# Attention outputs of a quad's two halves accumulated in one PSUM bank and evacuated once instead of twice

## The reference

```python
def _L0_attn_b_ref(x, qkv_w, qkv_b, out_w, out_b):
    H, hd = 16, 8
    qkv = (x @ qkv_w.T + qkv_b).reshape(B, S, H, 3 * hd)
    q, k, v = jnp.split(jnp.transpose(qkv, (2, 0, 3, 1)), 3, axis=2)
    scores = jnp.einsum('hbds,hbdt->hbst', q, k) / jnp.sqrt(jnp.float32(hd))
    w = jax.nn.softmax(scores, axis=-1)
    attn = jnp.einsum('hbst,hbdt->hbsd', w, v)
    ...
    return attn @ out_w.T + out_b
```

## Time and profile before

| | |
|---|---|
| median of 3 runs | 554.64 us |
| the profiled execution | 554.74 us |
| its span | 552.9 us |
| PE busy | 504.7 us (91%) |
| DVE busy | 461.9 us (84%) |
| ACT busy | 364.3 us (66%) |
| POOL busy | 101.7 us (18%) |

### The profile page before, as it was taken

How to read it: one execution, slowest core, us unless ns; L and a number is a source line. 1 busy time by engine, 2 the same in 40 slices (tenths; PEclk the granted TensorE clock), 3 DMA queues, 4 the chain that set the end, 5 groups by cost and what they waited for, 6 DMA issues and landing times.

```text
span 552.9 us, 9775 instructions
## 1 busy us (share of the span) xinstructions
PE 504.7 (91%) x3856; PEld 238.0 (43%) x3856; DVE 461.9 (84%) x649; ACT 364.3 (66%) x690; POOL 101.7 (18%) x122
## 2 busy tenths in 40 slices
PE   1994988998699999999999999999999999989797
PEld 1443465576334333333343333343343333333476
DVE  5999859987599899999999999999999999913753
ACT  1766230442101888888888888888888888898441
POOL 6974999241000000000000000000000000000000
PEclk9997989999755899999999999999999999999999
DMA  8111000004720030300300300300300000000001
GB/s 217 23 39 39 0 2 1 1 22 154 223 58 1 1 79 4 76 2 4 76 2 2 79 3 2 77 2 3 77 2 2 1 3 3 1 2 2 0 20 57
DMA packets 13786, 18.87 MB, mean 34 GB/s; under 512 B 3583, under 2 KB 10158, under 8 KB 12718
## 3 DMA queue, kind: packets, MB, share of 16 engines
q1 hardware_dynamic: 12888, 17.53, 12.1%
q0 software_dynamic: 304, 0.46, 0.5%
q10 hardware_dynamic: 550, 0.27, 0.2%
HBM read 11.70 MB, written 5.24 MB: 31 GB/s over the span
## 4 chain that ended last, share of the span: by engine, by line
PE 72%; DVE 16%; ACT 6%; DMA 3%; issue 2%; SPq 1%; ACTq 0%
PE ps L1295 27%; PE ps L1261 26%; PE pm L1031 6%; DVE acc L833 4%; PE pm L1218 3%; PE ps L1021 3%; PE pm L1021 3%; DVE mx L935 2%; ACT gate L690 2%; DVE h L749 2%; ACT o_sb L659 2%; PE ps L1245 2%; DMA kt<-k_scr 1%; DVE st L726 1%; DMA x<-in_L_attn_a_x 1%
## 5 line engine op out<-in xcount | busy, mean ns | idle before, releaser
L935 DVE TENSOR_REDUCE mx<-pm 128x1 f32<-128x1024 f32 x256 | 310.7, 1224 | 26.2 <-PE pm L1218 25.3
L1218 PE MATMUL pm<-kt,qt 62*128 62x512 f32 x512 | 198.8, 474 | 6.2 <-DVE mx L935 3.2
L1295 PE MATMUL ps<-qt,kt 64*128 64x512 f32 x496 | 182.6, 451 | 4.6 <-ACT gate L690 4.6
L690 ACT ACTIVATE gate<-ps 128x512 f32<-128x512 f32 x250 | 134.0, 599 | 17.4 <-PE ps L1295 16.1
L690 ACT ACTIVATE acc<-ps 128x512 f32<-128x512 f32 x246 | 133.7, 595 | 17.3 <-PE ps L1295 11.4
L1295 PEld LDWEIGHTS ps<-qt,kt 64*128 64x128 f32 x496 | 75.8, 186 | 99.8 <-ACT gate L690 45.3
L1218 PEld LDWEIGHTS pm<-kt,qt 62*128 62x128 f32 x512 | 82.8, 197 | 21.4 <-DVE mx L935 18.1
L1261 PE MATMUL ps<-gate,val 128*32 128x256 f32 x1024 | 82.4, 394 | 1.4 <-ACT gate L690 1.4
L1261 PE MATMUL ps<-acc,val 128*32 128x256 f32 x1024 | 78.5, 390 | 1.2 <-ACT acc L690 1.2
L478 POOL CAST mx_s<-mx 128x16 fp32r<-128x16 f32 x16 | 3.1, 196 | 273.5 <-DVE mx L935 273.5
L1261 PEld LDWEIGHTS ps<-acc,val 128*32 128x32 f32 x1024 | 21.8, 108 | 43.7 <-ACT acc L690 23.7
(11 more groups left out here) (193 smaller groups left out, 468.9 us busy)
## 6 DMA issues: line engine op xcount, KB each, us to landing
qt<-q_scr SPq DMA_DIRECT2D x32, 128.0 KB
kt<-k_scr SPq DMA_DIRECT2D x32, 128.0 KB
x<-in_L_attn_a_x SPq DMA_DIRECT2D x4, 256.0 KB, 4.8
us<-h SPq DMA_DIRECT2D x8, 128.0 KB, 2.4
q_scr<-attn SPq DMA_DIRECT2D x4, 256.0 KB, 2.8
k_scr<-attn SPq DMA_DIRECT2D x4, 256.0 KB, 4.1
q_scr<-gate SPq DMA_DIRECT2D x4, 256.0 KB, 2.7
k_scr<-gate SPq DMA_DIRECT2D x4, 256.0 KB, 3.9
```

The source lines that it names most:

```text
L690: act.activation(pexp[s % NPB][:, exp_heads(n, s)[j], :], e_bank(i), ACT.Exp, scale=SCALE).then_inc(exp_done, 1)
L935: dve.tensor_reduce(mx[:, hn % 2, u:u + 1], pm[g % MRING][:, :], AX.X, ALU.max).then_inc(m_read, 1)
L1218: mm = pe.matmul(pm[g % MRING][:, keys * CH:(keys + 1) * CH], qt[r][rows, half, pair, c * P:(c + 1) * P], kt[r][rows, keys, pair, :], star ...
L1295: pe.matmul(e_bank(i), keys, qt[r][rows, half, pair, :], start=True, stop=True).then_inc(exp_mm, 1)
```

## The change

The bank is now emptied once per quad. V is kept in rows of 41 columns (`VS = VW + HD + 1`): nine zeros, the 8 dimensions, the ones, and 23 zeros. `pv` still takes 32 columns of it as weights. In the first half it starts at column 9, so that the outputs and the sum stand in rows 0 to 8 of the head's 32 rows; in the second half it starts at column 0, so that they stand in rows 9 to 17, and nothing but zeros is added to rows 0 to 8. Both halves accumulate into the same 512 columns of bank 2, over all 16 steps. `copy_o`, `turn_o` and `copy_turned` run once per quad, at the first steps of the next quad; `copy_turned` issues two copies, one for each half's nine columns. The step s = 8 has the ordinary `ORDER`, and the ring of banks has one item less per quad. At the end VectorE copies both halves of the last quad.

```diff
--- before.py
+++ after.py
@@ -47,6 +47,7 @@
 SHIFT_ROW = ROWS - PARTS
 NBUF = 3
 VW = 32
+VS = VW + HD + 1
 EPS_LN, EPS_RMS = 1e-5, 1e-6
 SCALE = float(HD) ** -0.5
 STEPS = 2 * BT
@@ -97,7 +98,7 @@
 
     half, tile = divmod(s, BT)
     maxima = min(2 * NQ, 1 + 2 * n + half + ((tile, j) >= TURN_MAX_AT))
-    outputs = max(0, 2 * n - 1 + half + (tile >= TURN_O_AT))
+    outputs = max(0, n - 1 + (s >= TURN_O_AT))
     return (n * STEPS + s) * QH + j + maxima + outputs
 
 
@@ -113,9 +114,8 @@
     return exp_item(n, half * BT + TURN_MAX_AT[0], TURN_MAX_AT[1]) - 1
 
 
-def out_item(hn):
-    n, half = divmod(hn + 1, 2)
-    return exp_item(n, half * BT + TURN_O_AT, 0) - 1
+def out_item(n):
+    return exp_item(n + 1, TURN_O_AT, 0) - 1
 
 
 MORE_AT = (NQ - 1, LAST_UNIT_STEP + 2)
@@ -215,7 +215,9 @@
 
         qt = [sb(f"qt{r}", [P, 2, PAIRS, CH], F32R) for r in range(NBUF)]
         kt = [sb(f"kt{r}", [P, 2, PAIRS, CH], F32R) for r in range(NBUF)]
-        v4 = [val_f[:, r * BT * QH * VW:(r + 1) * BT * QH * VW].rearrange("p (c j w) -> p c j w", c=BT, j=QH)
+
+
+        v4 = [val_f[:, r * BT * QH * VS:(r + 1) * BT * QH * VS].rearrange("p (c j w) -> p c j w", c=BT, j=QH)
               for r in range(NBUF)]
 
         pexp = [gate[:, 0, :, :], gate[:, 1, :, :], acc[:, 0, :, :], acc[:, 1, :, :]]
@@ -450,7 +452,7 @@
                 pool.memset(v4[r][:, :, :, :], 0.0).then_inc(v4_zero, 1)
             pool.wait_ge(v4_zero, NBUF)
             for r in range(NBUF):
-                pool.memset(v4[r][:, :, :, HD:HD + 1], 1.0).then_inc(v4_ones, 1)
+                pool.memset(v4[r][:, :, :, 2 * HD + 1:2 * HD + 2], 1.0).then_inc(v4_ones, 1)
             pool.wait_ge(v4_ones, NBUF)
             for c in range(NCH):
 
@@ -465,7 +467,7 @@
                 if n >= NBUF:
                     pool.wait_ge(pv_mm, STEPS * (n - NBUF + 1))
                 src = v_tok[:, b * BT:(b + 1) * BT, :].rearrange("p c (g j d) -> p g c j d", g=GQ, d=HD)
-                pool.tensor_copy(v4[n % NBUF][:, :, :, 0:HD], src[:, g, :, :, :]).then_inc(v4_ready, 1)
+                pool.tensor_copy(v4[n % NBUF][:, :, :, HD + 1:2 * HD + 1], src[:, g, :, :, :]).then_inc(v4_ready, 1)
 
             def split_max(hn):
 
@@ -652,10 +654,10 @@
             first_parts(3)
 
 
-            def copy_o(hn):
-                act.wait_ge(pv_mm, hn * BT + BT)
-                if hn:
-                    act.wait_ge(exp_mm, out_item(hn - 1) + 1)
+            def copy_o(n):
+                act.wait_ge(pv_mm, n * STEPS + STEPS)
+                if n:
+                    act.wait_ge(exp_mm, out_item(n - 1) + 1)
                 act.activation(o_sb[:, :], bank(2), ACT.Copy).then_inc(o_copied, 1)
 
             def copy_max(hn):
@@ -665,26 +667,28 @@
                     act.wait_ge(shift_in, hn * SHIFT)
                 act.activation(nm_s[:, :], e_bank(max_item(hn))[0:PARTS * HT, 0:P], ACT.Copy).then_inc(exp_done, 1)
 
-            def copy_turned(hn):
-
-                n, half = divmod(hn, 2)
-                act.wait_ge(exp_mm, out_item(hn) + 1)
-                src = e_bank(out_item(hn)).rearrange("p (c j w) -> p c j w", c=TC, j=QH)
-                dst = attn[:, n, :, :].rearrange("p d (j c) -> p c j d", j=QH)[:, TC * half:TC * (half + 1), :, :]
-                act.activation(dst, src[:, :, :, 0:HD + 1], ACT.Copy).then_inc(exp_done, 1)
+            def copy_turned(n):
+
+                act.wait_ge(exp_mm, out_item(n) + 1)
+                src = e_bank(out_item(n)).rearrange("p (c j w) -> p c j w", c=TC, j=QH)
+                dst = attn[:, n, :, :].rearrange("p d (j c) -> p c j d", j=QH)
+                for half in range(2):
+                    ins = act.activation(dst[:, TC * half:TC * (half + 1), :, :],
+                                         src[:, :, :, (HD + 1) * half:(HD + 1) * (half + 1)], ACT.Copy)
+                ins.then_inc(exp_done, 1)
 
             def quad(n):
                 for s in range(STEPS):
                     half, tile = divmod(s, BT)
-                    if tile == TURN_O_AT and (n or half):
-                        copy_turned(n * 2 + half - 1)
+                    if n and s == TURN_O_AT:
+                        copy_turned(n - 1)
                     if n or s >= NPB:
                         act.wait_ge(pv_mm, n * STEPS + (s - NPB + 1))
                     for j in range(QH):
                         if (tile, j) == TURN_MAX_AT and n * 2 + half + 1 < 2 * NQ:
                             copy_max(n * 2 + half + 1)
-                        if (tile, j) == COPY_O_AT and (n or half):
-                            copy_o(n * 2 + half - 1)
+                        if n and (s, j) == COPY_O_AT:
+                            copy_o(n - 1)
                         i = exp_item(n, s, j)
                         act.wait_ge(exp_mm, i + 1)
                         act.activation(pexp[s % NPB][:, exp_heads(n, s)[j], :], e_bank(i), ACT.Exp,
@@ -696,7 +700,7 @@
                 act.wait_ge(scr_done[i], 2 * STORED)
             for n in range(NQ):
                 quad(n)
-            copy_o(2 * NQ - 1)
+            copy_o(NQ - 1)
 
             stds(3, 0)
             stds(3, 1)
@@ -936,7 +940,7 @@
 
             def sums(quads):
 
-                dve.wait_ge(exp_done, out_item(2 * quads[-1] + 1) + 1)
+                dve.wait_ge(exp_done, out_item(quads[-1]) + 1)
                 q = slice(quads[0], quads[-1] + 1)
                 settled(dve.reciprocal(o_rc[:, q, :], attn[:, q, HD, :]))
 
@@ -968,10 +972,13 @@
             projected(1)
 
             dve.wait_ge(o_turned, 1)
-            dve.wait_ge(exp_done, out_item(2 * NQ - 2) + 1)
             o = bank(4).rearrange("p (c j w) -> p c j w", c=TC, j=QH)
-            dst = attn[:, NQ - 1, :, :].rearrange("p d (j c) -> p c j d", j=QH)[:, TC:2 * TC, :, :]
-            settled(dve.tensor_copy(dst, o[:, :, :, 0:HD + 1]))
+            dst = attn[:, NQ - 1, :, :].rearrange("p d (j c) -> p c j d", j=QH)
+            for half in range(2):
+                dve.tensor_copy(dst[:, TC * half:TC * (half + 1), :, :],
+                                o[:, :, :, (HD + 1) * half:(HD + 1) * (half + 1)]).then_inc(dve_step, 1)
+            steps[0] += 2
+            dve.wait_ge(dve_step, steps[0])
             settled(dve.reciprocal(o_rc[:, NQ - 1, :], attn[:, NQ - 1, HD, :]))
             flatten(2, [GQ - 1])
             flatten(3, [GQ - 1])
@@ -1235,14 +1242,14 @@
                 pe.transpose(e_bank(max_item(hn))[0:PARTS * HT, 0:P], mx_s[:, hn % 2, :],
                              ident[:, :]).then_inc(exp_mm, 1)
 
-            def turn_o(hn):
-
-                pe.wait_ge(o_copied, hn + 1)
-                last = hn == 2 * NQ - 1
+            def turn_o(n):
+
+                pe.wait_ge(o_copied, n + 1)
+                last = n == NQ - 1
                 if not last:
-                    item_free(out_item(hn))
+                    item_free(out_item(n))
                 for t in range(TC):
-                    mm = pe.transpose((bank(4) if last else e_bank(out_item(hn)))[:, t * P:(t + 1) * P],
+                    mm = pe.transpose((bank(4) if last else e_bank(out_item(n)))[:, t * P:(t + 1) * P],
                                       o_sb[:, t * P:(t + 1) * P], ident[:, :])
                 mm.then_inc(o_turned if last else exp_mm, 1)
 
@@ -1253,14 +1260,14 @@
                     pe.wait_ge(exp_done, exp_item(n, s, QH - 1) + 1)
                     if s == 0:
                         pe.wait_ge(v4_ready, n + 1)
-                    hn = n * 2 + s // BT
-                    if s % BT == 0 and hn:
-                        pe.wait_ge(o_copied, hn)
+                        if n:
+                            pe.wait_ge(o_copied, n)
+                at = 0 if s // BT else HD + 1
                 cols = slice(part * (CH // 2), (part + 1) * (CH // 2))
                 for j in range(QH):
-                    mm = pe.matmul(bank(2)[VW * j:VW * (j + 1), cols], v4[r][:, s % BT, j, :],
-                                   pexp[s % NPB][:, j, cols], start=(s % BT == 0 and part == 0),
-                                   stop=(s % BT == BT - 1 and part == 1), tile_position=(0, VW * j))
+                    mm = pe.matmul(bank(2)[VW * j:VW * (j + 1), cols], v4[r][:, s % BT, j, at:at + VW],
+                                   pexp[s % NPB][:, j, cols], start=(s == 0 and part == 0),
+                                   stop=(s == STEPS - 1 and part == 1), tile_position=(0, VW * j))
                 if part == 1:
                     mm.then_inc(pv_mm, 1)
 
@@ -1277,12 +1284,12 @@
                     j = 0
                     if tile == 0:
                         pe.wait_ge(shift_in, (hn + 1) * SHIFT)
-                    if tile == TURN_O_AT and hn:
-                        turn_o(hn - 1)
+                    if n and s == TURN_O_AT:
+                        turn_o(n - 1)
                     if n == NQ - 1 and s in PROJECT_AT:
                         pe.wait_ge(m_read, UNITS)
```

(4 more changed lines are left out.)

## The result

| | before | changed |
|---|---|---|
| median of 6 runs | 554.78 us | 548.58 us |
| lowest to highest | 553.9 to 555.49 | 547.36 to 551.19 |
| the profiled execution | 554.74 us | 547.36 us |
| its span | 552.9 us | 545.6 us |

The ratio to the kernel before is 0.9892, 95% interval 0.9867 to 0.9916: 6 us faster. The kernel before has three runs more here than in the table ahead of the prediction. The forecast was 547.8, range 546.4 to 550.6. In the changed kernel's listing the lines stand a few numbers lower than before: L1295 is now L1302, L1218 is L1225, L1261 is L1268, L690 is L694, L935 is L939, L659 is L661, L1245 is L1252, L674 is L676, L974 is L978.

The account below looks back on a forecast made before the run. TensorE was taken to set the attention's pace, with VectorE some 7% in reserve. The terms -6.3 - 0.85 + 0.35 = -6.8 us led from the median of 554.64 to 547.8 us, range 546.4 to 550.6.

Parts of the forecast that it names:

- VectorE has a reserve and TensorE sets the pace: In the attention, VectorE can take a reduction per 1.14 us but gets one per 1.229; some 7% in reserve.
- 0.90 us per evacuation, seven times, -6.3 us: Inner evacuations of quads 0 to 6 go; each costs 0.44 + 0.59 - 0.13 = 0.90 us in the TensorE-paced stretch.
- Why the 0.44 us gap is there: VectorE's gap at a half boundary: TensorE waits 0.30 us for ScalarE, late because of the 0.60 us bank copy.
- -0.85 us in the last quad: Eighth inner evacuation, at 492 us with no maxima left: two steps' excess of 0.52 + 0.33; bounds 0.3 and 1.3.
- Second copy on ScalarE hidden, 0: Transposed output's second copy at seven outer boundaries adds 0.33 us of ScalarE time, covered: 0, at most 3.1 us.
- +0.35 us for the second copy at the end: At the attention's end VectorE copies two halves instead of one, on the path; bounds 0.2 and 0.41 us.
- Weight loads unchanged, 0: Loads of `pv` weights from 41-float rows at unaligned starts stay at 108 ns: 0, upper end 19.5 us.
- this rival: Padded V slows the first weight loads of 256 `pv` parts; 27 ns eats the gain, 76 ns gives 567.3 us; chance 0.05.
- GpSimd's longer memsets, 0: Memsets of V grow from 2.76 to 3.5 us, followed by 8.80 us of idle time, so nothing shows.
- its first rival: The doubled copy on ScalarE comes onto the path at outer boundaries: 550.9 us at worst, 549.3 at half; chance 0.08.

Follow-up runs that it names:

- e1_transposes: The changed kernel plus four 128x128 transposes on TensorE per quad, beside the maxima's transpose at step 5; ratio 0.9957 to the kernel before.
- e4_order_first: The changed kernel with the boundary order of letters kept at the inner boundaries, where nothing is emptied any more; ratio 0.9919 to the kernel before.

## Why the prediction was right, step by step

- **VectorE has a reserve and TensorE sets the pace**: right. e1_transposes adds TensorE time alone, and the expected 0.44 us a time appears as 0.43.
- **0.90 us per evacuation, seven times, -6.3 us**: right in size. In the same V layout it is 0.89, -6.2; the trace of the changed kernel shows -5.92, since the layout costs 0.28.
- **Why the 0.44 us gap is there**: wrong. I read the 0.30 us wait of TensorE as the lateness that the copy causes. Taking the copy away and keeping the order (e4_order_first) leaves the gap at 0.44 and the wait at 0.21. Two thirds of this part, 0.20 of 0.29, come from the order of letters and the ring of three banks. That this did no harm to the number is luck: the change removed the order along with the copy. Had the diff left `ORDER_FIRST` at s = 8, my sum would have been 1.4 us too good.
- **-0.85 us in the last quad**: right, 32.23 to 31.38. Half of it, 0.42, is the order here too (e4_order_first), which the prediction did not name.
- **Second copy on ScalarE hidden, 0**: right. The intervals across the outer boundary sum to the same; the cover is larger than I worked out.
- **+0.35 us for the second copy at the end**: the sign is right, it measured +0.25 (0.67 us for both copies instead of 0.41).
- **Weight loads unchanged, 0**: off by a little, +0.28 us, 1.3 ns for each part, where 27 ns would have taken the whole gain. The price of this rival was too low, though: I had counted one load of a part as exposed, 0.256 us for each ns that a load grows. The loads grew by 0.3 ns each and the part by 1.3, about four times as much. By this ratio, an estimate, loads longer by some 7 ns and not 27 would have eaten the gain.
- **GpSimd's longer memsets, 0**: nothing in the times of the paced stretch; no experiment was made on them alone.
- The sum was -6.8; from the 33rd reduction to the end -6.5 was measured, in the medians -6.2. Of the 0.3 between the first two, the V layout makes nearly all. The upper end of the range, 550.6, was set a little too low by the prediction's own sum: its first rival comes to 550.9 at worst.

## What to carry to other kernels

- An accumulator that uses 9 of 32 rows can take several results before it is emptied, by a window that slides over zero-padded weights. It cost no matmul time here, since the weights were 32 columns wide before too. Starts of the window on multiples of 16 bytes were 0.2 us better here than others. What it saves is each evacuation's time on the engine that sets the pace, here mostly the transposes with what hangs on them (0.60 of 0.89 us), and little the copy of the bank (0.09).
- A wait that ends with another engine's instruction isn't yet caused by that instruction. Before the cost is put down to it, ask whether the ring in front would have waited anyway; a run that keeps the order and leaves out the work tells it.
- Where two kernels run in lockstep with a regular pace, cut the traces at like instructions: differences of 0.2 us were clear there, while the whole times scattered by up to 4 us.
